# A Mamba-2 mixer with a small mixture-of-experts branch on one core: six places of a written-out instruction order are rearranged

## The reference, cut to what matters

```
proj = xn @ in_proj_w.T                      # 18560 channels: gate 8192, conv 10240, dt 128
hBC  = silu(causal_conv4(conv channels))     # heads 128x64, B 8x128, C 8x128
dt   = clip(softplus(dt + dt_bias), 0, 100)
# chunks of 128 tokens, 128 heads in 8 groups:
Y_diag = (C B^T * L) (hs*dt)                 # L = exp(segsum(dt*A)), lower triangle
states = B^T (decay * hs*dt), carried from chunk to chunk
Y_off  = C state * exp(A_cum)
g   = (Y_diag + Y_off + hs*D) * silu(gate)
out = rmsnorm over each 1024 channels(g) * norm_w @ out_proj_w.T
ffn = xn @ base_W.T + 2 * sum over top 2 of 8 experts of LoRA(xn)
result = x + out + ffn
```

## Time and profile before

| | us |
|---|---|
| median of 3 runs | 1626.4 (1622.24, 1626.4, 1627.02) |
| the profiled execution | 1625.32, its span 1624.0 |
| PE busy in the span | 1601.9 (99%) |
| POOL busy | 1337.9 (82%) |
| DVE busy | 1371.1 (84%) |
| ACT busy | 1253.0 (77%) |
| granted TensorE clock, mean | 0.996 of full |

### The profile page before, as it was taken

How to read it: one execution, slowest core, us unless ns; L and a number is a source line. 1 busy time by engine, 2 the same in 40 slices (tenths; PEclk the granted TensorE clock), 3 DMA queues, 4 the chain that set the end, 5 groups by cost and what they waited for, 6 DMA issues and landing times.

```text
span 1624.0 us, 31886 instructions
## 1 busy us (share of the span) xinstructions
PE 1601.9 (99%) x10792; PEld 1305.4 (80%) x10792; DVE 1371.1 (84%) x1665; ACT 1253.0 (77%) x2643; POOL 1337.9 (82%) x1240
## 2 busy tenths in 40 slices
PE   8998999999999999999999999999999999999999
PEld 7776888888888888888888888888888888888777
DVE  5978789887988879898798978988798887989788
ACT  5177787887878788787877878788787878778774
POOL 3157689996899879898799968999688987999796
PEclk9999999999999999999999999999999999999999
DMA  4162355554555554444645446545564465645453
GB/s 134 54 209 97 116 170 179 164 150 134 158 156 140 163 156 146 124 143 139 192 148 138 125 139 186 150 134 150 150 165 119 130 167 161 177 121 133 133 163 105
DMA packets 216387, 236.12 MB, mean 145 GB/s; under 512 B 154273, under 2 KB 155809, under 8 KB 212001
## 3 DMA queue, kind: packets, MB, share of 16 engines
q1 hardware_dynamic: 216224, 234.07, 50.3%
HBM read 147.51 MB, written 55.05 MB: 125 GB/s over the span
## 4 chain that ended last, share of the span: by engine, by line
PE 90%; DVE 4%; POOL 2%; issue 2%; ACT 1%; DMA 0%; SPq 0%; POOLq 0%; DVEq 0%; ACTq 0%
PE P L268 8%; PE P L269 8%; PE P L270 8%; PE P L514 8%; PE P L364 7%; PE P L347 7%; PE P L365 7%; PE P L371 7%; PE P L354 7%; PE P L348 7%; PE P L379 4%; PE P L500 2%; PE P L497 1%; PE P L498 1%; PE P L488 1%
## 5 line engine op out<-in xcount | busy, mean ns | idle before, releaser
L624 ACT ACTIVATE P<-AB,SC 128x128 f32<-128x128 f32 x1008 | 303.9, 360 | 20.6 <-DVE EM L1018 20.5
L268 PE MATMUL P<-xh,AH 128*128 128x512 f32 x656 | 263.4, 401 | 1.7 <-DVE hsX L887 1.5
L887 DVE SCALAR_TENSOR_TENSOR hsX<-P,cwt,hsX 128x1023 f32<-128x1023 f32 x189 | 241.7, 1279 | 26.8 <-ACT hsX L555 22.3
L269 PE MATMUL P<-xl,AH 128*128 128x512 f32 x656 | 256.9, 392 | 0.0
L270 PE MATMUL P<-xh,AL 128*128 128x512 f32 x656 | 256.8, 391 | 0.0
L347 PE MATMUL P<-GH,xh 128*128 128x512 f32 x512 | 211.7, 413 | 0.0
L364 PE MATMUL P<-OH,gTh 128*128 128x512 f32 x508 | 199.4, 392 | 2.5 <-issue 2.4
L348 PE MATMUL P<-GH,xl 128*128 128x512 f32 x512 | 200.8, 392 | 0.0
L365 PE MATMUL P<-OH,gTl 128*128 128x512 f32 x508 | 197.8, 389 | 0.0
L1245 POOL TENSOR_TENSOR AL<-AR,AH 128x512 fp32r<-128x512 f32 x82 | 110.3, 1345 | 80.6 <-ACT AH L542 80.6
L1274 POOL TENSOR_TENSOR DL<-dxh,DH 128x512 fp32r<-128x512 f32 x112 | 173.3, 1547 | 0.0
(11 more groups left out here) (229 smaller groups left out, 4174.8 us busy)
## 6 DMA issues: line engine op xcount, KB each, us to landing
AB<-acr_d SPq DMA_DIRECT2D x128, 512.0 KB, 4.7
half_d<-hsX SPq DMA_DIRECT2D x60, 512.0 KB, 3.7
AR<-in_wa SPq DMA_DIRECT2D x80, 256.0 KB, 2.7
TS<-in_wg SPq DMA_DIRECT2D x16, 1024.0 KB, 5.2
TS<-in_wo SPq DMA_DIRECT2D x16, 1024.0 KB, 6.7
part_d<-pl SPq DMA_DIRECT2D x64, 256.0 KB, 3.2
pl<-part_d SPq DMA_DIRECT2D x64, 256.0 KB, 3.6
SC<-sct_d SPq DMA_DIRECT2D x16, 128.0 KB, 5.2
```

Of the source, the lines that this page charges most:

```text
L268: te.matmul(o, ah_, bh_, start=(first and i == 0), stop=False)
L269: te.matmul(o, ah_, bl_, start=False, stop=False)
L624: r = se.activation(decays(m)[:, h, :], AB[m % 2][:, h, :], ACT.Relu, bias=SC[s % 2][:, c, 3, h:h + 1], scale=-1.0)
L887: ve.scalar_tensor_tensor(out=o[:, d:T], in0=raw[:, 0:T - d], scalar=cwt[:, n, 3 - d:4 - d], in1=o[:, d:T], op0=ALU.mult, op1=ALU.add).the ...
```

## The change

It moves instructions and takes none away; PE gets six more identity transposes.

1. PE's identity transposes at the start: 18 in place of 12.
2. ACT: `act_tanh(1)` goes behind the scalar copies of chunks 0 to 3 and the tap of tile 2.
3. ACT: the relus of slot 0 go ahead of the tanh of tile 4 and the first half tanh of tile 5; the ring copy `act_ring(9)` goes behind the exp of slot 0.
4. DVE: in slot 2 `dve_sum(2)` and `dve_gated(2)` go ahead of the convolution of tile 7, and the silu of tile 5's second half goes behind `dve_decay(2)`.
5. Slots 119 to 121: on DVE the decay of the next slot goes to the end of the slot; on ACT in slots 119 and 120 `gTh` goes ahead of the square and the output copy; of `GL` for head group 15 DVE makes two parts and POOL two (`s_gl3` counts DVE's).
6. Slot 122: `dve_output(120)` goes behind `dve_gated_lo(121)`, and `pool_rstd(120)` behind `pool_front(123)`.

```diff
@@ pe_gate
                 if s and k == 3:
                     te.wait_ge(s_gl3, s)
+                elif s == NS - 1 and k == 2:
+                    te.wait_ge(s_gl3, s + 1)
@@ pe_program
-            for i in range(12):
+            for i in range(18):
                 te.transpose(bank("X", 7)[:, 0:128], ident[:, :], ident[:, :])
@@ act_program
             act_ring(5)
-            act_tanh(1)
             se.wait_ge(s_acc0, NC)
             for c in range(NC):
                 if c == 4:
                     act_tap(2)
+                    act_tanh(1)
                     act_ring(6)
...
             act_tap5(0)
+            act_relus(0)
             act_tanh(4)
             act_tanh5(0)
-            act_relus(0)
-            act_ring(9)
             se.wait_ge(acc_st[5], 16)
             act_front(0)
             act_exp(0)
+            act_ring(9)
             act_input_hi(0)
...
+                bare = m in (M - 9, M - 8)
+                if bare:
+                    act_gated_hi(m - 1)
+                act_square(m - 1)
+                act_output(m - 2)
...
-                if m:
+                if not bare:
                     act_gated_hi(m - 1)
@@ dve_gate_lo
+            if s == NS - 1:
+                ve.wait_ge(s_gh, 4 * (1 + s) + 4)
+                ve.tensor_tensor(GL[:, 2, :], TS[:, 2, :], as_f(GH[:, 2, :]), ALU.subtract).then_inc(s_gl3, 1)
@@ dve_program
             dve_output_lo(0, 0)
-            dve_silu5(1)
             dve_output_lo(0, 1)
             dve_output_lo(0, 2)
             dve_decay(2)
+            dve_silu5(1)
...
-                for i in new_tiles:
+                for i in new_tiles if m > 2 else ():
                     dve_conv(i)
-                if not new_tiles and m + 1 < M:
+                bare = M - 9 <= m <= M - 7
+                if not new_tiles and m + 1 < M and not bare:
                     dve_decay(m + 1)
...
-                if m >= 2:
+                if m != M - 6:
                     dve_output(m - 2)
                 if m == M - 1:
                     dve_gated_lo(m - 1)
                 if m < M:
                     dve_sum(m)
                     dve_gated(m)
+                for i in new_tiles if m == 2 else ():
+                    dve_conv(i)
...
+                if m == M - 6:
+                    dve_output(m - 2)
+                if (new_tiles or bare) and m + 1 < M:
                     dve_decay(m + 1)
@@ pool_program
-                        pool_gate_lo(2 + s, (0, 1, 2))
-                if m >= 2:
+                        pool_gate_lo(2 + s, (0, 1, 2) if s + 2 < NS else (0, 1))
+                if m >= 2 and m != M - 6:
                     pool_rstd(m - 2)
...
                         pool_front(m + 1)
+                    if m == M - 6:
+                        pool_rstd(m - 2)
```

More of the change, by code:

```diff
@@ L853, in act_program @@
                     act_input_hi(m + 1)
-                if m:
-                    act_square(m - 1)
-                if m >= 2:
-                    act_output(m - 2)
+                bare = m in (M - 9, M - 8)
[3 more added lines that the diff above has]
+                act_output(m - 2)
                 if m < M and c == 1:
@@ L1235, in dve_program @@
                         dve_output_lo(s, 2)
-                if new_tiles and m + 1 < M:
+                if m == M - 6:
+                    dve_output(m - 2)
+                if (new_tiles or bare) and m + 1 < M:
                     dve_decay(m + 1)
@@ L1525, in sp_program @@
                 if m < M and c == 7 and s + 1 < NS:
-                    sp.wait_ge(s_gl, ngl(s + 2))
-                    sp.wait_ge(s_gl3, s + 1)
+                    sp.wait_ge(s_gl, ngl(s + 2) - (s + 2 == NS))
+                    sp.wait_ge(s_gl3, s + 1 + (s + 2 == NS))
                     sp.dma_start(TS[:, :, :], wo[s + 1]).then_inc(ts_in, 16)
```

## The result

| | before | changed |
|---|---|---|
| median, us | 1626.7 (6 runs, 1622.2 to 1628.0) | 1632.8 (6 runs, 1632.2 to 1633.9) |
| profiled execution, its span | 1625.3, 1624.0 | 1632.5, 1631.2 |
| PE busy | 1601.9 | 1602.3 |

The ratio is 1.0042, 95% interval [1.0029, 1.0055]: 6.8 us slower (4.7 to 8.9; the two medians lie 6.1 apart). The time is 2.0 us above the forecast of 1630.8.

What follows compares the result with a forecast made beforehand. PE, busy 99% of the span, was taken as the bound. Start -0.85 and tail +5.4 us sum to +4.5, on the median of 1626.4 giving 1630.9, stated as 1630.8; range 1620.5 to 1635.0 us.

Steps and rivals of the forecast that it cites:

- within 0.3%: Whole run: a time between 1621.5 and 1631.3 us, no change that a measurement can tell; chance 0.42.
- Edit 1: Start, PE: six more transposes cost 0.6 us, bounds 0 and 1.4.
- Edit 2: Start: PE loses a 2.8 us wait and a clock drop, 4.4 us, but waits elsewhere, so nothing gets through.
- Edit 3: Slot 0: later tanh and later `AL` on POOL make the state product 1.2 us late, bounds -0.5 and 2.3.
- Edit 4: Slot 2: tile 8's half starts 2.05 us sooner, clock drop stays; bounds -3.65 and -1.0.
- Start in all: Start: 1.2 less 2.05 gives -0.85 us, bounds -4.2 and +1.3.
- Edit 5: Slots 119 to 121, DVE: 1.1 us gained, 1.2 and 1.0 lost through the later decay of slot 122, sum +1.1.
- Edit 6: Slot 122: DVE idles 2.9 us for `rst(120)`, +3.0; PE waits 5 us for bank 4, clock drop adds 1.3.
- Tail in all: Tail: 1.1 + 3.0 + 1.3 = +5.4 us, bounds -3.3 and +7.
- Whatever is gained or lost in the start arrives at the tail in full: Slots 3 to 118: nothing changes and PE hardly waits, so the start's difference passes through whole.
- Rival (a): Tail: `rst(120)` is ready by 1573.2, both PE waits go (-3.3), start gives -2.35: 1620.7 us; chance 0.27.
- Rival (b): Start: waits ahead of `pe_front(0)` and slot 0's state product drop the clock too, start +1.3: 1634.6 us; chance 0.15.

Runs made afterwards that it cites:

- e11: Kernel before with only the edits of slots 119 to 122, start as before: 1630.0 us, ratio 1.0036.
- e12: Kernel before with the edits of slots 119 to 122, but `pool_rstd(120)` at its old place on POOL: 1627.0 us, ratio 1.0006.
- e5: Kernel before with 18 identity transposes in place of 12, nothing else: 1625.6 us, ratio 1.0002.
- e8: Kernel before with the changed start (transposes, scalar copies first, slot 2 moves), ACT's order around slot 0 as before: 1623.3 us, ratio 0.9989.
- e7: Kernel before with only the DVE moves in slot 2 (sum and gated early, silu behind the decay): 1623.1 us, ratio 0.9993.
- e6: Kernel before with only ACT's relus of slot 0 moved ahead and the ring copy moved behind the exp: 1626.6 us, ratio 1.0014.
- e10: Kernel before with sum and gated of slot 2 ahead of tile 7's convolution, the silu left ahead of the decay: 1621.8 us, ratio 0.9987.
- e2: Changed kernel with all edits of slots 119 to 122 undone, leaving the start's edits: 1627.8 us, ratio 1.0010.
- e1: Changed kernel with the slot 122 moves of `dve_output(120)` and `pool_rstd(120)` undone: 1629.3 us, ratio 1.0021.
- e9: Kernel before with only the edits of slots 119 to 121, except that the decay of slot 122 stays at its old place: 1624.1 us, ratio 1.0000.
- e4: Changed kernel with DVE's decays of slots 120 to 122 and silus back in their old places: 1631.6 us, ratio 1.0033.
- e3: Changed kernel with only `pool_rstd(120)` back at its old place on POOL: 1631.5 us, ratio 1.0034.

## Why the prediction was right, and where it was not

The time, 1632.8, lies in the range, and in the forecast's own range of 1627.5 to 1634.5; the forecast 1630.8 is 2.0 us too low, and "within 0.3%" had the largest chance where it came out 0.42% slower by the ratio. The mechanism that carries the sum, DVE waiting for `rst(120)` and PE for bank 4 behind it, is the one that was forecast, and e11 against e12 shows it by experiment. The start was forecast with the wrong sign and the tail 1.5 us too short in the trace; both errors point the same way, and the width of the range took them up. Step by step:

- **Edit 1**, +0.6: it can't be told from nothing (e5). Its bounds, 0 to 1.4, are in no bound of the start.
- **Edit 2**, nothing gets through: right. PE has no wait for the scalar copy, waits 2.5 us for a convolution at 94.66 in its place, and e8 is no faster than e7.
- **Edit 3**, part of +1.2: this term was **mis-sized**. The mechanism is as described: relus released by the DMA of `EA` (after 4.24 us of idle time on ACT, at 102.73, forecast 103.2), tanh at 105.09 (105.6), `AL` at 111.37 (111.6), `DL` alone at 1.27 us (1.3). But `AL` took 1.87 us, not the 1.30 of the earlier trace rows, and what I called 1.2 us with edit 1's remnant in it is 1.9 us by itself, 2.3 by the ratio of e6. The 1.2 is not what its own terms add up to either: 2.1 less 1.0 is 1.1, and that leaves 0.1 for edit 1 and the 0.5 ahead of `pe_front(0)`.
- **Edit 4**, -2.05: the step that failed is "whose queue moves by 0.1 us only, since the tanh of tile 6 now waits for the later silu". That tanh moved by 2.7 us against the state of slot 0, and the relus of slot 3 and the tap behind it by 1.2. I had seen the wait and not what is queued behind it. The bound "-1.0 if the tap comes 1 us later" is what came: -0.9 by the start of tile 8's half, -1.1 by the ratio. With the silu left in place (e10) the forecast is nearly met: 146.65 less 113.93 = 32.7 us, measured 33.0. The wait of PE is 2.7 us, as forecast, though most of it is for bank 4, and the clock fell behind it, as forecast.
- **Start in all**, -0.85: measured +1.6 (0 to 3.3) by e2. The sign is wrong, and the value lies just outside the bounds (+1.3), though its interval reaches into them.
- **Edit 5**, +1.1 for DVE: **mis-sized**. Less the 0.7 us that the changed profile had lost by slot 115, PE's state product of slot 123 is 1.1 us late, but on DVE the decay of that slot (1571.78, before 1569.10) is 2.0 late. By the ratios of e1 and e2 edit 5 costs 1.8, by their tails 3.4; of these 3.4, 0.6 was lost ahead of slot 119, and some 1.6 goes with the clock that fell in slot 123.
- **Edit 6**: DVE idle 3.07 us (forecast 2.9), PE 4.92 us (5), the drop of the clock, all as named. The gate of slot 123 came 0.8 us later than reckoned (1580.17, or 1579.47 on the clock of the kernel before, for 1578.7): `SL` starts at 1572.31, 1571.6 on the clock of the kernel before, where I had put about 1570.6. `SH` stands on ACT behind the relus of slot 123, and these waited 3.92 us for the decay that edit 5 had moved; I had charged that lateness to the decay of slot 123 and not to `SH`. `L948` took 1.47 us, between the 1.78 that I kept and the 0.74 of the shortest `L945` of the kernel before; it started 0.13 us behind POOL's `xch(124)` (1577.88 to 1578.92).
- **Tail in all**, +5.4: 6.9 in the trace (6.5 to the end of the span), 5.9 by e11.
- "Whatever is gained or lost in the start arrives at the tail in full": **false**, see below.

Rival (a) needed `rst(120)` in time; e12 is that case, and it gives no gain at all in the tail: PE's wait ahead of `pe_output(121)` is 1.85 us there and not zero. As I read it with e9, the -3.3 that I put on PE's two waits isn't to be had while DVE sets the pace. (Its -2.35 for the start should be -2.45, 1.2 less 3.65.) Rival (b) named the right culprit, `AL`, but its own sign did not come: `DL(0)` ended at 115.46, not after 116.5, and the start cost 1.6 us by e2 where (b) had 2.9. The second drop of the clock did not come in the changed kernel's profile, but it did in that of e2, which has the same start: 0.57 from 116 to 120 us, and 9.81 us from the state of slot 0 to that of slot 1.

## What to carry to other kernels

Before moving a producer and its consumer to the end of their queues together, ask which queue is longer: here the consumer's place on DVE cost little and the producer's, behind four instructions of POOL that wait for a copy of ACT, cost 3.2 us in the traces of one start and 4.9 by the ratios of the other (though only 1.3 by the ratios of the first, which is unexplained). A wait that moves takes along everything queued behind the waiting instruction; go down that queue to the end (twice here, `tanh(6)` and the relus of slot 123, the second item was priced at 0.1 and 0.4 us late and was 1.2 and 1.4). And a gain ahead of a stretch where another engine is full may be worth nothing: of the 1.3 us that e9 won up to the state of slot 121, 1.1 was gone by slot 124.

## What the runs showed of the hardware

**A shift of 0.15 us decides who pays for a collision.** In slot 34 DVE's silu and POOL's sum start together. Before, DVE is first, by 0.03 us, and POOL pays:

```profile
522.31 1.22 DVE L915 SCALAR_TENSOR_TENSOR hsX<-th,hsX 128x1024 f32<-128x1024 f32 x1
```

```profile
522.34 2.34 POOL L1372 TENSOR_TENSOR al<-al,dhs 128x512 f32<-128x512 f32 x1
```

After, POOL is first, by 0.01, and DVE pays, and PE stands still 22 us later, for a result of DVE:

```profile
522.16 2.36 DVE L918 SCALAR_TENSOR_TENSOR hsX<-th,hsX 128x1024 f32<-128x1024 f32 x1
```

```profile
522.15 1.30 POOL L1383 TENSOR_TENSOR al<-al,dhs 128x512 f32<-128x512 f32 x1
```

```profile
544.13 0.50 PE L366 MATMUL P<-OH,gTh 128*128 128x512 f32 x1 [0.54 <-DVE Gt L997]
```

The Trainium skill, page "SBUF — State Buffer", section "Who interferes with whom", says that a DVE instruction with two SBUF inputs contends with a GpSimd instruction that reads SBUF, that the lock is exclusive, and that the order of issue decides who blocks. The trace agrees: 1.22 us becomes 2.36 when POOL is first, and 1.30 becomes 2.34 when DVE is. What I had not expected is the sum of it. From slot 3 to slot 115 all kernels run the same program, and yet the stretch is 1342.2 us in six of the fourteen profiles, one such step of 0.85 us longer in three (1343.05, 1343.09, 1343.09), two in e1 (1343.94) and four in e4 and e10 (1345.6); e3 and e6 have odd ones (1343.25, 1342.76). All the whole steps lie between the states of slots 19, 35, 51, 67, 83 or 99 and the next, sixteen slots apart; the changed kernel's follows the collision shown. A gain in the start can be lost there, or the reverse.

**The same stall may or may not drop the clock.** With the same instructions up to slot 118, the changed kernel is granted 0.59 behind its wait in slot 2 (its row stands with the result), and e3 is not slowed at all:

```profile
148.00:152.00 4.00, 3.67 (x18) 2.91 (x17) 3.41 (x4) 2.40 (x4) 4.00 (x4) 1.00 0.01 4
```

The cleanest pair is e11 and e12, the same program up to slot 122. Each waits 1.55 us (1.54) for a convolution in slot 1; behind it, e11 first:

```profile
122.00:126.00 4.00, 4.00 (x48) 3.17 (x47) 3.14 (x6) 1.82 (x5) 4.00 (x3) 1.00 0.21 49
```

```profile
122.00:126.00 4.00, 4.00 (x32) 3.01 (x32) 3.32 (x6) 1.67 (x3) 4.00 (x3) 0.66 0.22 66
```

From the state of slot 1 to that of slot 2 it takes 14.05 us in e11 and 15.57 in e12. All fourteen profiles have this wait, 1.54 or 1.55 us; nine then take 14.0 us with the clock at 1.00, and five 15.6 with 0.89 in the mean. So a drop costs 1.6 us, as the prediction had it, but the program does not decide whether it comes. Slots 0 to 3 take 40.8 to 44.7 us in the five profiles with the changed start, by where and how often the clock falls. With the steps above this is enough for the spread of the runs of one kernel (the kernel before, in the hours of e1 to e4: 1622.2 to 1628.5). So a difference of 2 us between two profiles says little; that of one stretch, with its clock beside it, says much.
